# The recurrence's stores move from SP's queue to POOL's

## The reference, cut to what matters

```python
def step(carry, kv_t):                      # wkv_scan, for each pixel t
    p, q, o = carry
    no = jnp.maximum(o, u + kt)
    A, Bw = jnp.exp(o - no), jnp.exp(u + kt - no)
    y = (A * p + Bw * vt) / (A * q + Bw)
    no2 = jnp.maximum(w + o, kt)
    A2, B2 = jnp.exp(w + o - no2), jnp.exp(kt - no2)
    return ((A2 * p + B2 * vt, A2 * q + B2, no2), y)
...
k, v, r = (einsum('btc,dc->btd', xs, W) for W in (Wk, Wv, Wr))
x_fwd = wkv_scan(real_w, u, k, v)
x_bwd = flip(wkv_scan(real_w, u, flip(k), flip(v)))
h = sigmoid(r) * 0.5 * (x_fwd + x_bwd)
out = einsum('btc,dc->btd', layernorm(h) * ln_g + ln_b, Wo)
```

## Time and profile before

| | us |
|---|---|
| three runs | 7094.77, 7114.15, 7173.1 |
| median | 7114.15 |
| profiled execution | 7110.93 |
| its span, first to last instruction | 7109.3 |
| VectorE busy | 5427.1 |
| TensorE busy | 5460.2 |
| POOL busy | 350.9 |

### The profile page before, as it was taken

The page is one execution under the profiler, slowest core; times in us unless marked ns, Lnnn a source line. Parts: engine busy times, 40 slices in busy tenths (PEclk is TensorE's granted clock), DMA queues, the critical chain, the costliest instruction groups (busy, mean ns, idle before and its releaser), DMA issues. The chain is left out here.

```text
span 7109.3 us, 79983 instructions
## 1 busy us (share of the span) xinstructions
PE 5460.2 (77%) x25018; PEld 2253.5 (32%) x25018; DVE 5427.1 (76%) x4277; ACT 2777.6 (39%) x3511; POOL 350.9 (5%) x555
## 2 busy tenths in 40 slices
PE   0999999799998676456566677769957887995887
PEld 0333333343333366233333222222222222221222
DVE  6333333799999787888887566659989995998998
ACT  0222222111212286211111000018867775886776
POOL 0111110000000000122221000000000000000000
PEclk9999999899999787677777788879988888997888
DMA  8566555999999999699998899966667774665775
GB/s 303 175 194 194 178 192 179 243 278 268 274 271 272 237 236 236 147 250 248 251 253 217 214 265 268 267 177 240 244 233 248 266 257 143 245 250 220 266 266 208
DMA packets 1178672, 1665.82 MB, mean 234 GB/s; under 512 B 82308, under 2 KB 902213, under 8 KB 1148741
## 3 DMA queue, kind: packets, MB, share of 16 engines
q1 hardware_dynamic: 836165, 1364.55, 63.2%
q10 hardware_dynamic: 314880, 201.39, 10.2%
q0 software_dynamic: 27520, 98.54, 5.4%
HBM read 1006.55 MB, written 657.67 MB: 234 GB/s over the span
## 5 line engine op out<-in xcount | busy, mean ns | idle before, releaser
L508 PE MATMUL dw_p<-dw_it,dw_tt 128*128 128x512 f32 x2304 | 1028.1, 608 | 119.9 <-DVE dw_tt L424 82.1
L547 DVE SCALAR_TENSOR_TENSOR dw_vo<-dw_vi,keep_wv,dw_vo 128x2048 f32<-128x2048 f32 x384 | 903.1, 2352 | 13.6
L842 PE MATMUL bc_p<-bc_z,bc_wc 128*32 128x256 f32 x9216 | 572.7, 414 | 395.8 <-DVE bc_z L881 395.8
L320 PE MATMUL pw_p<-pw_xh,pw_wlo 128*112 128x512 f32 x1536 | 694.7, 602 | 185.2 <-POOL pw_xh L274 185.2
L881 DVE STREAM_TRANSPOSE bc_z<-bc_xp 128x1536 f32<-128x1536 f32 x256 | 711.0, 2851 | 151.0 <-DMA bc_xp<-d 146.1
L1090 PE MATMUL ap_p<-ap_vt,ap_pw 96*96 96x512 f32 x1024 | 590.1, 742 | 184.3 <-DMA ap_xt<-in_x 181.2
L508 PEld LDWEIGHTS dw_p<-dw_it,dw_tt 128*128 128x128 f32 x2304 | 443.0, 194 | 705.1 <-issue 674.0
L525 ACT ACTIVATE dw_ot<-dw_p 128x512 f32<-128x512 f32 x384 | 216.0, 599 | 931.8 <-PE dw_p L508 658.9
L375 DVE COPY pw_ut<-pw_p 112x512 f32<-112x512 f32 x384 | 247.5, 686 | 379.4 <-PE pw_p L326 377.3
L842 PEld LDWEIGHTS bc_p<-bc_z,bc_wc 128*32 128x32 f32 x9216 | 319.7, 119 | 648.9 <-issue 483.4
L820 ACT ACTIVATE bc_xt<-bc_p 128x256 f32<-128x256 f32 x384 | 147.7, 385 | 870.2 <-PE bc_p L842 870.2
(11 more groups left out here) (317 smaller groups left out, 8464.9 us busy)
## 6 DMA issues: line engine op xcount, KB each, us to landing
u<-pw_ut SPq DMA_DIRECT2D x64, 2240.0 KB, 12.7
dw_it<-u SPq DMA_DIRECT2D x192, 512.0 KB, 10.8
d<-dw_ot ACTq DMA_DIRECT2D x192, 512.0 KB, 12.1
gr_qk<-d SPq DMA_DIRECT2D x128, 768.0 KB, 9.0
bb_d<-wb_bb SPq DMA_DIRECT2D x64, 1536.0 KB, 5.2
wf_bb<-bb_d SPq DMA_DIRECT2D x64, 1536.0 KB, 7.4
bc_xp<-d SPq DMA_DIRECT2D x256, 288.0 KB, 12.0
bc_xp<-d POOLq DMA_DIRECT2D x256, 288.0 KB, 9.8
```

The costliest lines, as they stand in the source:

```text
L320: mm(pt[m % NBANK][e][:, :], wlo[:, wm], xh[:, h, 2 * e, cols], start=True, stop=False, skip_group_check=True)
L508: mm = nc.tensor.matmul(po[c][:, :].rearrange("p (b w) -> p b w", b=B), tt[:, h, 3 * c + dx, 0:H], it[:, h, B * c:B * (c + 1), dx:dx + W], ...
L547: nc.vector.scalar_tensor_tensor(vo[:, h], src, w, vo[:, h], ALU.mult, ALU.add).then_inc(tapped, 1)
L842: mm = nc.tensor.matmul(po[q % NBANK][32 * c4:32 * c4 + 32, :, :], wc[:, c, dx, :, :].rearrange("p j r -> p (j r)"), z[:, h, c, :, dx:dx + ...
```

## The change

The three stores of the backward pass and the four of the forward pass are issued by POOL. The waits in front of them are the same, and so are their order among themselves, their sizes and the semaphores they raise. SP keeps the loads, the store of the maxima and the waits at the end of a stage. Line numbers below L1336 stay; those of the stores in the changed kernel are L1352, L1355 and L1359.

```diff
--- before.py
+++ after.py
@@ -1333,17 +1333,6 @@
                     wait(sp, r_done, n - 1)
                     own_wait(sp, passed)
                     tile_loads(sp, xt[:, h], x1, pair, bass.ds(chunk(n) * CH, CH), loaded[h])
-                if has(n, 1):
-                    sp.wait_ge(bv_done, n)
-                    own_wait(sp, passed)
-                    sp.dma_start(rows_of(bb_d, chunk(n - 1)), bb[:, 1 - h].rearrange("p a b t -> p (a b t)")).then_inc(b_stored[1 - h], 16)
-                    sp.wait_ge(tg_done, n)
-                    own_wait(sp, passed)
-                    sp.dma_start(rows_of(tg_d, chunk(n - 1)), flat(tg[:, 1 - h])).then_inc(g_stored[1 - h], 16)
-                if has(n, 4):
-                    sp.wait_ge(y_done, n - 3)
-                    own_wait(sp, passed)
-                    sp.dma_start(rows_of(y_d, chunk(n - 4)), flat(yb[:, h])).then_inc(y_stored[h], 16)
             wkv_steps(sp, step)
             sp.wait_ge(m_done, NCH)
             sp.dma_start(mx_d, mx[:, :, :]).then_inc(mx_stored, 16)
@@ -1352,6 +1341,23 @@
                 sp.wait_ge(b_stored[h], 16 * (NCH // 2))
                 sp.wait_ge(y_stored[h], 16 * (NCH // 2))
                 sp.wait_ge(g_stored[h], 16 * (NCH // 2))
+
+        @block.gpsimd
+        def _(pool):
+
+            def step(n, h, t):
+                if has(n, 1):
+                    pool.wait_ge(bv_done, n)
+                    own_wait(pool, passed)
+                    pool.dma_start(rows_of(bb_d, chunk(n - 1)), bb[:, 1 - h].rearrange("p a b t -> p (a b t)")).then_inc(b_stored[1 - h], 16)
+                    pool.wait_ge(tg_done, n)
+                    own_wait(pool, passed)
+                    pool.dma_start(rows_of(tg_d, chunk(n - 1)), flat(tg[:, 1 - h])).then_inc(g_stored[1 - h], 16)
+                if has(n, 4):
+                    pool.wait_ge(y_done, n - 3)
+                    own_wait(pool, passed)
+                    pool.dma_start(rows_of(y_d, chunk(n - 4)), flat(yb[:, h])).then_inc(y_stored[h], 16)
+            wkv_steps(pool, step)
 
         @block.tensor
         def _(pe):
@@ -1564,10 +1570,6 @@
                     wait(sp, o_done, n - 3)
                     own_wait(sp, passed)
                     tile_loads(sp, xr[:, h], x1, pair, bass.ds((n - 2) * CH, CH), r_loaded[h])
-                if has(n, 5):
-                    sp.wait_ge(ev_done, n - 4)
-                    own_wait(sp, passed)
-                    tile_stores(sp, out, xo[:, g], pair, bass.ds((n - 5) * CH, CH), stored[g])
             wkv_steps(sp, step)
             for h in range(2):
                 sp.wait_ge(stored[h], 64 * (NCH // 2))
@@ -1690,6 +1692,14 @@
                 pool.wait_ge(ones_made, k + 2)
                 nc.gpsimd.memset(oneb[64 * k:64 * k + 64, 64 * k:64 * k + 64], 1.0 / C).then_inc(ones_made, 1)
 
+            def step(n, h, t):
+                g = 1 - h
+                if has(n, 5):
+                    pool.wait_ge(ev_done, n - 4)
+                    own_wait(pool, passed)
+                    tile_stores(pool, out, xo[:, g], pair, bass.ds((n - 5) * CH, CH), stored[g])
+            wkv_steps(pool, step)
+
         @block.vector
         def _(dve):
             nc.vector.memset(wo[:, WD:WN], 0.0).then_inc(cleared, 1)
```

## The result

The changed kernel takes 7142.09 us in the median of its runs (7126.53 to 7162.51), against 7114.65 us for the kernel before in runs beside it, twenty of each. The ratio is 1.0038 with a 95% interval of 1.0023 to 1.0052: 27 us slower, which the many runs show, though it is under 1%. The forecast was 7116 us with 7085 to 7165 around it.

A forecast was written before the change was run, and what follows sets the result against it. VectorE was taken to bound the passes, busy 2034.23 of 2063.01 us. Passes were counted as zero and the four ends as 2 x 1.7 + 2 x 0.9 = +5.2 us on 7110.93, giving 7116 us, range 7085 to 7165.

The forecast's parts named there:

- The steady state doesn't change: Inside the passes: scan windows again 490 and 541 us, scans at 6.63 us; forecast with its ends given 0.88.
- SP's freed list is worth nothing: In the passes: earlier loads remove most of TensorE's 15.3 us wait on wb_xt per backward pass, but gain zero.
- POOL gains 247 us of issue, all hidden: In the passes: 448 issues of 0.55 us each on POOL, otherwise idle there, add zero to the path.
- bb_d may land 21.1 us after its issue: Backward pass, tightest store: landing took 5.2 us, leaving 15.9 us to lose; bounded at 19.0 us, so zero cost.
- rival A: Backward pass: POOL's stores starve, bb_d lands too late and holds up its buffer; 208 us, 7324 us, chance 0.05.
- Rival B: In the passes: VectorE is held while POOL prepares each DMA; 247 us on the path, 7363 us, chance 0.04.
- Rivals C and D: C: SP's freed list speeds the passes, 7087 us, 0.03. D: stores don't move or keep their times, 7111 us, under 0.01.
- The four ends cost 5.2 us together: Ends of passes: slower issue and about 1 us later landing by POOL, +1.7 us forward, +0.9 us backward, twice each.
- The prediction's own sign: At the four ends: a cost of 5 us or more each would show the assumed 1 us of lateness wrong.
- The upper end of +46 us: At the four ends: upper bound of their sum, from the convolution stage's slowest landing, 13.8 us against 2.2.

The follow-up runs named there:

- experiment 2: The kernel before, with only the stores of each pass's last chunk issued by POOL: 7114.89 us, ratio 0.9999 to the kernel before.
- 5: The changed kernel with one more DRAIN on POOL in each stage, ahead of the last chunk's stores: 7120.82 us, ratio 1.0005 to the kernel before.
- 1: The changed kernel, but SP issues the stores of each pass's last chunk: 7114.01 us, ratio 0.9997 to the kernel before.
- 4: The changed kernel, but POOL waits for its last stores to land before it drains: 7149.88 us, ratio 1.0059 to the kernel before.
- 7: The changed kernel with only every second chunk's stores on POOL, the others on SP: 7131.69 us, ratio 1.0017 to the kernel before.
- 9: The changed kernel with five stores per forward chunk, 160 DMAs in a forward stage: 7128.39 us, ratio 1.0020 to the kernel before.
- 10: The changed kernel with three stores per forward chunk, two joined, 96 DMAs in a forward stage: 7132.87 us, ratio 1.0028 to the kernel before.
- 3: The changed kernel with the backward stages' stores back on SP, only the forward ones on POOL: 7125.99 us, ratio 1.0013 to the kernel before.

## Why the prediction was right where it was, and wrong where it was not

**The time lay in the range, the sum of the ends did not hold.** The number was 26 us too low. By the steps:

- *The steady state doesn't change*: right. 2062.72 for 2063.01 us, scans still 6.63 us.
- *SP's freed list is worth nothing*: right. The loads of wb_xt now go out at 5006.83 with bb_d at 5010.88, and TensorE's wait on them is gone from the pass; its wait for ScalarE there grew from 20.3 us to 37.3 in its place, and VectorE's only wait on TensorE is still 0.3 us, as the earlier trace rows:

```profile
DVE wb_mx L1458 <- PE wb_p L1216: 0.3, 1, 0.3
```
```profile
PE wb_p L1210 <- ACT wb_bb L1401: 37.3, 29, 1.6
```

- *POOL gains 247 us of issue, all hidden*: right for the passes, 241.5 us in all. The step went on to put POOL's part of the path at zero because "POOL has nothing else to do there". It didn't ask whether an issued DMA leaves POOL work for later, and that is where the failed sum below begins.
- *bb_d may land 21.1 us after its issue*: never near. The rows that answer to the earlier trace rows:

```profile
bb_d<-wb_bb POOLq DMA_DIRECT2D x64, 1536.0 KB, 5.5
wf_bb<-bb_d SPq DMA_DIRECT2D x64, 1536.0 KB, 8.2
```

5.5 us for SP's 5.2, and the load of bb in the forward pass has 8.2 for 7.4. So rival A (starving stores) is refuted: the 13.8 us of the earlier trace rows say nothing of stores in the passes. Nor was the empty queue there as good a match for VectorE's memset as I took it for: the memset ended at 2911.04, and the first packet of POOL's queue went at 2913.39. By the rule of the Trainium skill, "SBUF — State Buffer", section "SBUF: two separate sides", a store behind a locking VectorE instruction would have to wait for its end; with VectorE busy 99% of the pass the trace shows 0.3 us more, so the scans and the two-operand instructions here did not lock POOL out to any such degree.
- *Rival B (POOL slows VectorE)*: refuted, 2033.90 us of VectorE's work for 2034.23 with 220.93 us of POOL's beside it.
- *Rivals C and D*: refuted. No pass became faster, and POOL issues all 448.
- *The four ends cost 5.2 us together*: this step failed, and it is the term of the sum that was mis-sized: 30.4 us measured. I had written that the last stores land later by about 1 us and are issued 0.18 us slower each. What this stands for was right in size, 4 us measured for the 5.2: POOL begins its issue 0.5 us later than SP, its four issues take 0.3 us more in all and not 0.7, and the landings came 0.3 to 0.4 us later. That experiment 2 shows 5.2 us to the digit is chance. What the sum left out is POOL's DRAIN at the end of a stage, 8.47 us in the backward and 11.40 us in the forward stages. It ends 4.8 and 8.2 us after SP's last wait. Less the 0.4 us in which the barrier followed before, that is 2 x 4.6 + 2 x 8.0 = 25 of the 30.4 us; the rest is the 4 us of the stores and the scatter of the forward ends. I had asked only when the data arrives, and not what the issuing engine has to do before it reaches the barrier. The prediction's own sign came true ("if the ends cost 5 us or more each"): they cost 5.4 to 10.4. But it would have blamed the 1 us, and the fault was the missing term. The upper end of +46 us came from another mechanism, a landing as late as the slowest in the convolution stage, and held the time by its width alone: that the time lay in the range was luck.

How sure is the cause? It is shown from both sides: the DRAIN made short by an earlier one (5), hidden by a later end on SP (1), moved back by a wait (4), and scaled by the count in 7 (forward), 9 and 10. What POOL does during a DRAIN isn't in the trace; "clearing a list" is my picture of it. Open are the 1.1 us of experiment 7 and the 1.3 us of 9, the 1.6 us at the forward ends in 3, and what sets the number of DMAs between two stops, 128 for these stores and 108 for the loads of the convolution stage.

## What to carry to other kernels

A store that is moved to POOL's queue costs POOL about 0.54 us of issue at once, and about 0.08 us later, at the next DRAIN (measured after 96 and 128 DMAs). Where a stage ends in a barrier right behind POOL's last DMA, let another queue issue the last ones, or drain POOL earlier beside other work. When a chain of waits at a stage's end names only the barrier, look at the queues' own rows of the line that closes the stage: the DRAIN that ends last is what all engines wait for, and a long one that is hidden today is a price for the next change.

## What the runs showed of the hardware that I had not expected

- POOL's DRAIN takes 0.082 us for each DMA that it has issued since the last one, by count and not by size (7.90 us after 96, 10.51 after 128, all landed).
- That grows only up to a limit. After 128 stores the 129th waits 3.1 us, and a DRAIN is short again (3.1 us for 8 issued behind the second such stop, 4.8 for 32 behind the first). The second stop came 120 DMAs later, and the loads of the convolution stage stop before the 114th, 222nd and 330th, for 2.7 us.
- A DRAIN of POOL also waits for the landing of what it issued: 3.3 to 3.7 us at an idle end, 7.8 to 8.9 us in a pass (landing there: 7.6 us for out, 7.7 for y_d).
- 48.9 us of POOL's issue in a backward pass left it at 489.94 us for 490.02, though VectorE is 99% busy in it.
